# A two-layer decoder on one core: linear attention's sums of squares and key products summed by TensorE, keys scaled for the state update by ScalarE

## What is computed

```
qkv = (x @ Wqkv.T).reshape(B, T, 3, H, DH)          # B 8, T 128, H 16, DH 8
q, k = l2norm(qkv[:, :, 0]), l2norm(qkv[:, :, 1]);  v = qkv[:, :, 2]
alpha, beta = sigmoid(x @ Wg.T + bg), sigmoid(x @ Wb.T + bb)
def step(S, inp):                                    # scanned over T, S is DH x DH per (b, h)
    Sk = einsum('bhij,bhj->bhi', S, k_t)
    S = a*(S - b*Sk[..., :, None]*k_t[..., None, :]) + b*v_t[..., :, None]*k_t[..., None, :]
    o = einsum('bhij,bhj->bhi', S, q_t)
out = outs.reshape(B, T, D) @ Wout.T
```

## Time and profile before

| | |
|---|---|
| median of 3 runs | 394.66 us (394.35 to 398.3) |
| the profiled execution | 393.56 us |
| its span | 391.2 us |
| mean granted TensorE clock | 0.96 |
| PE busy | 323.8 us, 83% |
| DVE busy | 314.4 us, 80% |
| POOL busy | 217.5 us, 56% |
| ACT busy | 214.2 us, 55% |

### The profile page before, as it was taken

One profiled execution on the slowest core, in us unless ns is written; L12 is line 12 of the kernel. 1 busy time (PEld: TensorE's weight loads), 2 busy tenths in 40 slices (PEclk: granted clock), 3 DMA queues, 4 the chain that ended last, 5 costly groups with the idle time before them and its releaser, 6 DMA issues. The chain is left out here.

```text
span 391.2 us, 5322 instructions
## 1 busy us (share of the span) xinstructions
PE 323.8 (83%) x1680; PEld 227.2 (58%) x1680; DVE 314.4 (80%) x638; ACT 214.2 (55%) x468; POOL 217.5 (56%) x223
## 2 busy tenths in 40 slices
PE   5537929779778789878998997988799989999992
PEld 2332428778545455522343585555598857989872
DVE  0899999998676885999999999999957724763934
ACT  2636032231144938849769636786565656675741
POOL 3499999996214050379899989888702610100111
PEclk9958959999999989999999999999999999999997
DMA  8900000000000001425334453545300000000000
GB/s 259 418 10 1 0 3 0 2 1 2 0 2 0 0 1 21 137 89 157 142 131 148 132 152 98 165 135 136 91 1 2 0 0 0 3 3 0 2 27 27
DMA packets 11521, 24.41 MB, mean 62 GB/s; under 512 B 1231, under 2 KB 2255, under 8 KB 11239
## 3 DMA queue, kind: packets, MB, share of 16 engines
q1 hardware_dynamic: 11495, 24.09, 19.3%
HBM read 23.50 MB, written 0.59 MB: 62 GB/s over the span
## 5 line engine op out<-in xcount | busy, mean ns | idle before, releaser
L1085 POOL TENSOR_TENSOR arena<-arena 128x512 f32<-128x512 f32 x63 | 80.0, 1280 | 29.9 <-DVE arena L707 27.9
L707 DVE TENSOR_TENSOR_SCAN arena<-arena,ps 128x512 f32<-128x512 f32 x64 | 77.1, 1207 | 0.0
L1344 ACT ACTIVATE arena<-arena,neg_a 128x508 f32<-128x508 f32 x64 | 43.3, 711 | 7.5 <-DVE arena L707 6.7
L700 DVE TENSOR_TENSOR ps<-arena,ps 128x512 f32<-128x512 f32 x64 | 43.2, 676 | 1.1 <-PE ps L1775 0.9
L1126 POOL TENSOR_TENSOR rstd<-veps,mhalf 128x4 f32<-128x4 f32 (+2 forms) x6 | 4.8, 810 | 68.8 <-DVE veps L836 35.8
L1621 PE MATMUL ps<-arena,first_in 128*128 128x128 f32 (+1 forms) x256 | 31.5, 285 | 13.1 <-POOL arena L959 13.1
L744 DVE TENSOR_REDUCE arena<-ps 128x2 f32<-128x496 f32 x32 | 21.4, 668 | 25.1 <-PE ps L1841 25.0
L1621 PEld LDWEIGHTS ps<-arena,first_in 128*128 128x128 f32 x256 | 30.5, 200 | 14.4 <-issue 8.2
L1794 PE MATMUL ps<-arena,first_in 128*128 128x512 f32 x64 | 33.5, 605 | 1.4 <-POOL arena L1085 1.3
L1775 PE MATMUL ps<-arena,pick_wide 96*128 96x512 bf16 x64 | 24.5, 386 | 11.6 <-DVE arena L707 11.1
L1394 ACT ACTIVATE first_in<-ps 128x256 f32<-128x256 f32 x32 | 12.4, 387 | 33.2 <-PE ps L1867 33.1
(11 more groups left out here) (294 smaller groups left out, 837.5 us busy)
## 6 DMA issues: line engine op xcount, KB each, us to landing
arena<-c_rows_dram SPq DMA_DIRECT2D x64, 256.0 KB, 3.2
fold_in<-in_fold_dram SPq DMA_DIRECT2D x1, 2056.0 KB, 10.9
late_in<-in_late_dram SPq DMA_DIRECT2D x1, 1423.5 KB, 16.3
early_in<-in_early_dram SPq DMA_DIRECT2D x1, 921.5 KB, 12.8
xres<-in_x_dram SPq DMA_DIRECT2D x1, 512.0 KB, 13.3
kv_ctx<-in_context_dram SPq DMA_DIRECT2D x1, 480.0 KB, 6.8
first_in<-in_first_dram SPq DMA_DIRECT2D x1, 465.0 KB, 3.8
rows_in<-in_rows_dram SPq DMA_DIRECT2D x1, 384.0 KB, 13.8
```

Source lines behind the costliest of these rows:

```text
L700: tt(chain(q), dtu[:, n, cols(g)], chain(q), ALU.mult).then_inc(S("drive"), 1)
L707: nc.vector.tensor_tensor_scan(hist[:, q % NBUF], fade[:, q % NFADE], chain(q), 0.0, ALU.mult, ALU.add).then_inc(S("scan"), 1)
L1085: tt(seen[:, q % NBUF], hist[:, q % NBUF], c_wide[:, q % NBUF], ALU.mult).then_inc(S("read_out"), 1)
L1344: act(fade[:, q % NFADE].rearrange("p (b t) -> p b t", t=T)[:, :, 1:], dt[:, n, cols(g)].rearrange("p (b t) -> p b t", t=T)[:, :, 1:], ACT ...
```

## The change

Squares are taken by ScalarE from `qkvt` before the turning (seven batches; VectorE takes the eighth), and TensorE turns them with accumulation, so that the sum over 8 dimensions arrives in PSUM. The sigmoid's table is loaded earlier. VectorE multiplies the key products before it scales v, from the largest group to the smallest, and TensorE sums them as it does the query products; VectorE applies the decays in 7 parts. `Kend` is gone: ScalarE scales the keys by 128 activations of 8 elements. ScalarE's other work is reordered around them.

```
+            ve.wait_ge(S("qkv_odd"), B // 2)
+            tt(sq[:, :, B - 1], qkvt[:, 0:2 * DH, B - 1], qkvt[:, 0:2 * DH, B - 1], ALU.mult).then_inc(S("square_last"), 1)
...
-                nc.vector.tensor_reduce(norm2[n], square[...].rearrange("p (t j) -> p t j", j=DH),
-                                        AX.X, ALU.add).then_inc(S("square_sum"), 1)
...
+            ve.wait_ge(S("unit"), 2)
+            ve.wait_ge(*after("k_ps", 1))
+            cell_of = {i: NC * i * (i - 1) // 2 for i in range(1, C)}
+            for i in range(C - 1, 0, -1):
+                rows = gram_k[:, cell_of[i] * DH:(cell_of[i] + NC * i) * DH].rearrange("p (c i j) -> p c i j", i=i, j=DH)
+                tt(rows, Kc[:, :, i:i + 1, :].to_broadcast([P, NC, i, DH]), Kp[:, :, 0:i, :], ALU.mult).then_inc(S("gram_k"), 1)
...
-            for t in range(1, C):
-                step(nc.vector.tensor_reduce(low[:, :, t, 0:t], rows_k[t - 1], AX.X, ALU.add))
-            tt(low, low, bdecay, ALU.mult).then_inc(S("low_ready"), 1)
+            ve.wait_ge(S("low_mm"), 1)
+            for i in range(C - 1, 0, -1):
+                cells = bank(5)[:, cell_of[i]:cell_of[i] + NC * i].rearrange("p (c i) -> p c i", i=i)
+                tt(low[:, :, i, 0:i], cells, bdecay[:, :, i, 0:i], ALU.mult).then_inc(S("low_ready"), 1)
... GpSimd
-            tt(Kend, Kc, decay[:, :, C - 1, :].unsqueeze(3).to_broadcast([P, NC, C, DH]), ALU.mult).then_inc(S("k_end"), 1)
... ScalarE
+            def key_ends(chunks):
+                for c in chunks:
+                    for i in range(C):
+                        ins = act(kend_ps[:, c, :, i], K[:, c * C + i], ACT.Copy, scale=decay[:, c, C - 1, i:i + 1])
+                return ins
+            ac.wait_ge(S("w_start"), 1)
+            ac.wait_ge(S("beta_v"), 1)
+            act(w_ps[:, own], X[:, own, :, DH:], ACT.Copy).then_inc(S("w_ps"), 1)
+            ac.wait_ge(S("gram_k"), C - 1)
+            key_ends(range(NC // 2))
+            for g in range(2):
+                ac.wait_ge(S("fold_qk_mm"), 4 * (g + 1))
+                act(fold_qk[:, 4 * g:4 * g + 4], ..., ACT.Copy).then_inc(S("fold_qk"), 1)
+            key_ends(range(NC // 2, NC)).then_inc(S("kend_ps"), 1)
... TensorE
+            for n in range(2):
+                if n:
+                    pe.wait_ge(S("gates"), 2)
+                for j in range(DH):
+                    ins = mm(norm2[n], sq[:, (1 - n) * DH + j].rearrange("p b h -> p (b h)"), ident, is_transpose=True,
+                             start=(j == 0), stop=(j == DH - 1))
+                ins.then_inc(S("square_sum"), 1)
...
+            pe.wait_ge(S("unit"), 1)
+            stay_awake(6, 5)
+            for i in range(C - 1, 0, -1):
+                pe.wait_ge(S("gram_k"), C - i)
+                for j in range(DH):
+                    ins = mm(bank(5)[:, cells_of[i]:cells_of[i] + NC * i], ident, rows[:, :, j], start=(j == 0), stop=(j == DH - 1))
+            ins.then_inc(S("low_mm"), 1)
```

More of the change, by code:

```diff
@@ L57 @@
 RIDES = {
-    "ctx_root": ("square", 2),
-    "k_ps": ("square", 3),
+    "ctx_root": ("square", B - 1),
+    "k_ps": ("square", B),
     "ctx_back": ("v_turned", 1),
@@ L180, in decoder @@
         qkvt = A(B * (3 * D + 2 * H)).rearrange("p (n b h) -> p n b h", b=B, h=H)
-        square = A(2 * T * DH)
+        sq = A(2 * DH * P).rearrange("p (n b h) -> p n b h", b=B, h=H)
         end = A.at
@@ L190, in decoder @@
         A.at = max(A.at, solved)
-        Kend = A(T * DH).rearrange("p (c t j) -> p c t j", t=C, j=DH)
         NP = 4
@@ L452, in _ @@
             ts(cveps[0:TC], cmv[0:TC, :, 1], EPS, None, ALU.add).then_inc(S("ctx_var"), 1)
[L454 to L458, removed]
-                                        AX.X, ALU.add).then_inc(S("square_sum"), 1)
-                ve.wait_ge(S("square_sum"), n + 1)
-                ts(norm2[n], norm2[n], 1e-24, None, ALU.max).then_inc(S("floored"), 1)
+            floored(1)
             for n, dst in ((0, K), (1, Q)):
@@ L1145, in columns_out, with squared @@
                     ACT.Copy).then_inc(S("xcol"), 1)
+            def squared(b):
+                act(sq[:, :, b], qkvt[:, 0:2 * DH, b], ACT.Square).then_inc(S("square"), 1)
             for b in range(0, B, 2):
@@ L1149, in _ @@
                 act(qkvt[:, :, b], bank(b)[:, 0:3 * D + 2 * H].rearrange("p (n h) -> p n h", h=H), ACT.Copy).then_inc(S("qkv_even"), 1)
+                if b == 0:
+                    ac.wait_ge(S("second_in"), 16)
+                    table_of(ACT.Sigmoid)
+                else:
+                    ac.wait_ge(S("qkv_even"), b // 2)
+                    squared(b - 2)
+                    ac.wait_ge(S("qkv_odd"), b // 2)
+                    squared(b - 1)
+            ac.wait_ge(S("qkv_even"), B // 2)
+            squared(B - 2)
             ac.wait_ge(S("gates_turned"), 1)
@@ L1162, in _ @@
                     act(crstd[0:TC], cveps[0:TC], ACT.Sqrt).then_inc(S("ctx_root"), 1)
[L1164 removed]
+            ac.wait_ge(S("unit"), 1)
             act(k_ps, K, ACT.Copy).then_inc(S("k_ps"), 1)
[L1166 to L1171 removed]
             ac.wait_ge(S("ctx_rstd"), 1)
@@ L1590, in _ @@
             ins.then_inc(S("gates_turned"), 1)
+            pe.wait_ge(S("square"), B - 1)
+            pe.wait_ge(S("square_last"), 1)
+            for n in range(2):
[5 more added lines that the diff above has]
+                ins.then_inc(S("square_sum"), 1)
             for n, (k, sem) in ((0, (1, "kq_turned")), (1, (0, "kq_turned")), (3, (2, "v_turned"))):
@@ L1595, in _ @@
                 ins.then_inc(S(sem), 1)
+            pe.wait_ge(S("unit"), 1)
+            stay_awake(6, 5)
+            cells_of = {i: NC * i * (i - 1) // 2 for i in range(1, C)}
+            for i in range(C - 1, 0, -1):
+                rows = gram_k[:, cells_of[i] * DH:(cells_of[i] + NC * i) * DH].rearrange("p (n j) -> p n j", j=DH)
+                pe.wait_ge(S("gram_k"), C - i)
+                for j in range(DH):
+                    ins = mm(bank(5)[:, cells_of[i]:cells_of[i] + NC * i], ident, rows[:, :, j], start=(j == 0), stop=(j == DH - 1))
+            ins.then_inc(S("low_mm"), 1)
             pe.wait_ge(S("fold_in"), 16)
```

40 lines of the change are left out of this document (11 added, 29 removed).

## The result

The changed kernel takes 403.64 us (median of four, 401.81 to 403.77), the kernel before 394.5 us in the same session. The ratio is 1.0229, with a 95% interval of 1.0187 to 1.0272: slower, by 9.1 us in the medians. The interval lies wholly above 1, on both sides of 2%.

A forecast was written before the change was run, and what follows sets the result against it. VectorE looked like the bound, but ScalarE's last copy of `att` gates both loops. Front (-2.5) and VectorE savings (about -5) end in waits; +10.2 us takes 393.56 to 403.8, with the median 1.1 above: 404.8 us, range 401.2 to 409.5.

The forecast's parts named there:

- The place: ScalarE's last copy of `att`, which starts both loops over chunks, moves from 49.63 to 59.9: +10.2 us.
- The front: Start up to `Q`: first reciprocal from 18.26 to 15.8, `Q` ready at 20.4, 2.5 us earlier.
- Key sums: TensorE's seven groups of 16 records take 15.6 us, replacing VectorE reductions of 4.24 us.
- The clock: TensorE's last key-sum group and folding run at half clock: sums end at 38.9, folding at 42.4.
- the rival whose clock stays at 1.00: TensorE's sums end at 37.2, folding at 39.0, query sums at 57.2: +7.6, 402.3 us; chance 0.22.
- The turns hold the clock: TensorE before `stay_awake`: full clock should hold; if not, everything is 1.6 us later, 406.4 us, chance 0.05.
- ScalarE's keys: 128 activations of 8 elements at 0.20 us each; ScalarE is done 0.7 us before TensorE.
- The query sums and the copies of the folded weights: TensorE's query sums wait for folding and ScalarE's 0.60 us copy, start at 43.1, complete `att_mm` at 59.8.
- The substitution: On VectorE, after seven small products: starts at 40.0, ends at 53.9; `solved` is there long before the last copy.
- loops that absorb part of the shift: Sign of a wrong prediction: the loops behind the last copy of `att` take up part of its shift.
- Not slower: TensorE's sums keep pace with VectorE's products; last copy of `att` moves 1.2 us: 395.9 us, no change; chance 0.05.

The follow-up runs named there:

- e4: Changed kernel with `gram_k` laid out dimension by dimension, so that TensorE's key sums read packed; 402.35 us, ratio 1.0233 to the kernel before.
- e6: Changed kernel with the seven groups of key products and sums in rising order of size; 403.94 us, ratio 1.0234 to the kernel before.
- e5: Changed kernel with v scaled and the weights folded and copied out ahead of the key sums; 400.33 us, ratio 1.0145 to the kernel before.
- e11: Changed kernel with folding ahead of the key sums, query products packed and scaled keys on GpSimd; 402.47 us, ratio 1.0189 to the kernel before.
- e9: Kernel before plus early squares summed by accumulating turns, and query products laid out so that TensorE reads packed; 391.87 us, ratio 0.9959.
- e1: The front alone: kernel before plus only squares ahead of the turning and 16 accumulating turns; 391.84 us, ratio 0.9969.
- e2: Changed kernel with key sums back on VectorE, ScalarE's 128 key activations kept; 401.6 us, ratio 1.0202 to the kernel before.
- e7: Kernel before plus early squares with accumulating turns, scaled keys by one VectorE product into PSUM, and packed query products; 396.85 us, ratio 1.0053.
- e10: Kernel before plus early squares with accumulating turns, packed query products, keys of chunks 0 to 7 on ScalarE, rest on GpSimd; 390.49 us, ratio 0.9922.

## Why the prediction was right, point by point

- **The place.** "The whole sum below is how far L1194's last copy moves." It moved by 10.27 us, with 10.2 forecast, but 0.88 of it is this execution's late first data: that the two numbers agree is luck. Without it the shift is 9.4, the medians differ by 9.1, and the forecast of 404.8 is 1.2 us high.
- **The front.** First reciprocal at 16.59, 15.7 without the late start, forecast 15.8. `Q` at 20.35 on that clock, forecast 20.4. The turns of the squares took 1.94 us, forecast 1.9.
- **Key sums.** Forecast 15.6 us at full clock, measured 16.0 (22.40 to 38.45). Strided large groups cost 0.20 us a record, small ones 0.11; e4 showed that stride and record floor are two limits, as argued.
- **The clock.** I took the last group and the folding at half clock. The folding was: 3.76 us instead of about 2. The last group was so only in the last quarter of its records, and took about 2.2 us instead of 3.5. That is most of what the forecast was high by, and the time lies between the forecast and the rival whose clock stays at 1.00 (402.3 us). e6 and e5 show the folding at full clock when it stands behind full columns or early.
- **The turns hold the clock.** 1.00 from 15 to 17 here, with 21 turns in the window. The Trainium skill ("TensorE: Matmul & The Clock Gate", Part 4: PE-mode transpose) says that the full clock does not engage for transposes. The trace differs and decides, for fp32 turns.
- **ScalarE's keys.** 0.192 us each, forecast 0.20. The estimate by the price in the Trainium skill ("ScalarE: Activation LUTs", What ACT_TABLE_LOAD costs) was 193 ns: the trace agrees. ScalarE was ready for the last copy 1.5 us before TensorE, forecast 0.7.
- **The query sums and the copies of the folded weights.** Start at 42.95, 42.1 without the late start, forecast 43.1: the 1.0 us that the clock gave. They took 16.9 us, forecast 16.8.
- **The substitution.** 39.80 to 53.68, forecast 40.0 to 53.9, and long done when the last copy ran, as forecast.
- **Not foreseen.** In the profiled execution 1.65 us came back at 145 to 158, where the clock fell before and not after. The prediction counted each us of the shift as a us of the total. It named loops that absorb part of the shift as a sign of being wrong; they absorbed none (94.21 to 104.47), and it was a later stage, in this execution, that did.

The rival that ended on the other side ("Not slower") needed records that average under 0.11 us and keys under 0.14; they took 0.14 and 0.19.

## What to carry to other kernels

Work moved off the busiest engine is worth what the next chain allows, so find the instruction where the chains meet and price the work in its new place, in that engine's own order. A sum over 8 that VectorE did in 4.2 us took TensorE 16, because a matmul record has a floor that few columns don't use, and a strided operand a rate that the clock doesn't lift. The same small activations that lengthened a chain on the path cost nothing in ScalarE's idle time and made the fastest version.

## What the runs showed of the hardware

- A fp32 matmul record with 128x128 weights starts about 0.11 us after the last at full clock, with 16 columns (e6: 16 records in 2.0 us) or with 112 packed ones (e4: 16 in 2.0 us), and 0.21 to 0.23 at half (e4: 16 records of 16 columns in 3.6 us).
- Every eighth fp32 element as the moving operand: 448 columns take 0.8 us a record at either clock; packed, the whole of the query sums fell from 16.9 to 9.6 us (e11).
- The granted clock fell from 1.00 to 0.50 while TensorE issued without a gap: at 37.6 in the changed kernel, between 31 and 33 in e4 and at 27.6 in e6, each time within groups of 48, 32 or 16 columns or just behind them. In e6 it stayed at 0.50 through the groups of 64, 80 and 96.
- VectorE's products writing with a stride of 1792 bytes took 6.45 us instead of 4.27. GpSimd's, with a stride of 2304 bytes, took 11.91 (e9) against 11.85 packed (e1): no cost.
- VectorE's product of 1024 elements took 1.23 us with one operand in PSUM. With both in SBUF it took 1.93 to 2.81, and in all seven traces that have it beside GpSimd (before, e1, e2, e7 to e10) it ended 1.08 to 1.09 us after the GpSimd product then under way. GpSimd's next product, if it began meanwhile, was about 1.0 us longer. GpSimd's `Kend`, 2.98 us before and 1.97 in the front alone, is such a case: in the front alone the last query product carries that us (3.35 against 2.36).
